# Second attention's first rows loaded within its projections, plain norms in two groups over eight banks, second chunk of each feed-forward turned later

## Time and profile before

| | |
|---|---|
| median of 3 runs | 1845.64 us (1845.48 to 1847.41) |
| profiled execution | 1844.86 us, span 1843.1 us |
| PE busy | 1647.8 us, 89% |
| DVE busy | 1372.2 us, 74% |
| ACT busy | 1104.0 us, 60% |
| POOL busy | 690.9 us, 37% |
| mean granted PE clock | 0.959 |

### The profile page before, as it was taken

One profiled execution on the slowest core, in us unless ns is written; L12 is line 12 of the kernel. 1 busy time (PEld: TensorE's weight loads), 2 busy tenths in 40 slices (PEclk: granted clock), 3 DMA queues, 4 the chain that ended last, 5 costly groups with the idle time before them and its releaser, 6 DMA issues. The chain is left out here.

```text
span 1843.1 us, 43046 instructions
## 1 busy us (share of the span) xinstructions
PE 1647.8 (89%) x14612; PEld 1021.5 (55%) x14612; DVE 1372.2 (74%) x2840; ACT 1104.0 (60%) x2096; POOL 690.9 (37%) x804
## 2 busy tenths in 40 slices
PE   2799999999999999999947664899999999985897
PEld 1477777787777778777724332233333333323555
DVE  4487887887788788778776574888888888846674
ACT  4566666666666666666646541366666666675452
POOL 0655554555555455555330432021212121223012
PEclk9999999999999999999979867899999999997999
DMA  4321121122112112211100020000000000000001
GB/s 129 96 56 44 43 54 40 43 48 54 43 43 54 40 43 48 52 44 34 24 1 1 6 101 12 15 14 14 15 14 15 14 15 14 10 1 1 1 12 35
DMA packets 53109, 61.86 MB, mean 34 GB/s; under 512 B 11345, under 2 KB 32018, under 8 KB 53010
## 3 DMA queue, kind: packets, MB, share of 16 engines
q1 hardware_dynamic: 53010, 60.55, 13.5%
HBM read 18.57 MB, written 2.10 MB: 11 GB/s over the span
## 5 line engine op out<-in xcount | busy, mean ns | idle before, releaser
L1732 ACT ACTIVATE a_prob<-psum 128x1024 f32<-128x1024 f32 (+3 forms) x384 | 302.3, 813 | 212.1 <-PE psum L1689 209.5
L1772 DVE TENSOR_REDUCE a_mx<-psum 128x1 f32<-128x512 f32 (+3 forms) x608 | 367.6, 655 | 61.5 <-PE psum L1671 55.6
L1764 POOL TENSOR_SCALAR_AFFINE_SELECT a_prob<-a_prob 128x256 f32<-128x256 f32 x256 | 103.9, 406 | 420.5 <-ACT a_prob L1732 418.1
L1668 PE MATMUL psum<-a_kd,a_qp 128*128 128x512 f16 (+3 forms) x768 | 218.3, 339 | 33.8 <-DMA a_kd<-a_k_part 23.0
L498 POOL TENSOR_TENSOR a_swp<-a_swp,a_sin 128x512 f32<-128x512 f32 x128 | 163.2, 1275 | 163.7 <-DMA a_swp<-a_lin 163.7
L854 DVE TENSOR_REDUCE a_nmax<-psum 128x1 f32<-128x1024 f32 (+7 forms) x256 | 191.4, 748 | 1.0 <-PE psum L569 1.0
L726 ACT ACTIVATE a_prob_big<-psum,a_nmax 128x1024 f32<-128x1024 f32 (+3 forms) x128 | 121.9, 953 | 103.3 <-DVE a_nmax L854 101.5
L502 POOL TENSOR_TENSOR a_rope<-a_swp,a_cosd 128x512 f32<-128x512 f32 x128 | 164.1, 1282 | 12.4 <-POOL a_swp L498 4.8
L1668 PEld LDWEIGHTS psum<-a_kd,a_qp 128*128 128x128 f16 x768 | 70.7, 98 | 173.9 <-DVE a_mx L1772 94.4
L1710 PE MATMUL psum<-a_prob,a_vg 128*32 128x512 f32 (+3 forms) x1536 | 165.4, 503 | 0.7 <-ACT a_o_sb L1738 0.3
L849 DVE TENSOR_TENSOR a_pt_lo_big<-psum,a_pt_hi_big 128x512 f16<-128x512 f32 (+3 forms) x256 | 138.5, 582 | 30.2 <-ACT a_pt_hi_big L721 30.2
(11 more groups left out here) (279 smaller groups left out, 4434.3 us busy)
## 6 DMA issues: line engine op xcount, KB each, us to landing
a_swp<-a_lin SPq DMA_DIRECT2D x256, 128.0 KB, 2.3
a_qp<-a_q_part SPq DMA_DIRECT2D x192, 16.0 KB
a_kd<-a_k_part SPq DMA_DIRECT2D x192, 16.0 KB
x<-_attn_hidden_states_dram SPq DMA_DIRECT2D x4, 512.0 KB, 5.6
a_w_raw<-in_L_attn_Wq_dram SPq DMA_DIRECT2D x16, 128.0 KB, 2.3
a_w_raw<-in_L_attn_Wk_dram SPq DMA_DIRECT2D x16, 128.0 KB, 2.3
a_w_raw<-in_L_attn_Wv_dram SPq DMA_DIRECT2D x16, 128.0 KB, 2.3
a_wo_raw<-in_L_attn_Wo_dram SPq DMA_DIRECT2D x1, 2048.0 KB
```

The costliest lines, as they stand in the source:

```text
L1668: last = pe.matmul(to[:, j * n:(j + 1) * n], qp[:, w % 3, t * P:(t + 1) * P], kd[:, w % 3, j0 + j, a:e], start=True, stop=not edge)
L1732: act.activation(prob_at(u, i)[:, 2 * pair:2 * pair + 2, a % BANK:a % BANK + e - a], c.psum[:, pair_of(u, i):pair_of(u, i) + 2, 0:e - a], ...
L1772: dve.tensor_reduce(mx[:, t, j0:j0 + per, a // BANK], work(("S", w, i))[:, 0:per * (e - a)].rearrange("p (j n) -> p j n", j=per), AX.X, AL ...
```

## The change

Three edits.

1. The 24 DMAs of unit 0 leave the attention block and are issued in the projections block, once the zeroing and the line of -1 are done and six low parts (those of sequence 0) are there. The attention block's SP loop begins at unit 1. `loaded_qk` is made earlier for that.
2. `boundary`, `Norm`, `run_steps` and the unused options of `Extra` go. The plain norms become `norm_and_turn`, written out without loops: the statistics chain runs for two groups, tiles 0 to 3 and tiles 4 to 15; each pair of tiles has a bank of its own, and the scaled tiles have four slots of two. `Moments`, which the feed-forwards already used, moves up in the file unchanged.
3. In chunk 0 of each feed-forward, the turn of chunk 1 with its high and low parts comes after ht = HT - 2 (4 in f0, 6 in f1) instead of ht = 2, on all three engines.

```diff
+    FIRST = TPC
+    NP = NT // 2
+        xn = c.sb(f"{name}_xn", [P, 4, 2, D], F32, ctx)
+        norm = Moments(c, name, [(0, FIRST), (FIRST, NT)], ctx)
...
+                norm.statistics(dve, c.x, 0, FIRST)
+                norm.variance(dve, 0)
+                norm.statistics(dve, c.x, FIRST, 2 * FIRST)
+                norm.normaliser(dve, 0)
+                norm.statistics(dve, c.x, 2 * FIRST, NT)
+                norm.variance(dve, 1)
+                norm.normaliser(dve, 1)
+                for m in range(NP):
+                    low(m)
...
+                def scale(m):
+                    act.wait_ge(norm.norm_ready, 2 if 2 * m < FIRST else 4)
+                    wait(act, turned, m - 3)
+                    for t in (2 * m, 2 * m + 1):
+                        act.activation(xn[:, m % 4, t % 2:t % 2 + 1, :], c.x[:, t:t + 1, :], ACT.Identity, ...)
...
+                norm.root(act, 0)
+                scale(0)
+                scale(1)
+                high(0)
+                high(1)
+                norm.root(act, 1)
+                for m in range(2, NP + 1):
+                    if m < NP:
+                        scale(m)
+                    if m >= 3:
+                        high(m - 1)
...
+                for m in range(NP):
+                    pe.wait_ge(xn_ready, 2 * m + 2)
+                    for j in range(2):
+                        for k in range(KT):
+                            last = pe.transpose(c.psum[:, m, k * 2 * P + j * P:k * 2 * P + (j + 1) * P],
+                                                xn[:, m % 4, j, k * P:(k + 1) * P], c.ident[:, :])
+                    last.then_inc(turned, 1)
...
+    TURN_AT = [HT - 2] + [2] * (CHUNKS - 1)
-                        if ht == 2 and ch + 1 < CHUNKS:
+                        if ht == TURN_AT[ch] and ch + 1 < CHUNKS:
...
+                @block.sync
+                def _(sp):
+                    sp.wait_ge(zeroed, 2)
+                    sp.wait_ge(lined, J)
+                    sp.wait_ge(lo_done, CB * NJ)
+                    load_rows(sp, 0)
...
-                    for u in range(NU):
+                    for u in range(1, NU):
...
+                        load_rows(sp, u)
```

More of the change, by code:

```diff
@@ L122, in wait, with __init__ @@
         eng.wait_ge(sem, value)
[L125 to L140, removed]
+class Moments:
     STEPS = 9
-    def __init__(self, c, name, ctx, unit=1.0):
-        self.eps = EPS * unit * unit
-        sb = lambda n, *shape: c.sb(f"{name}_{n}", [P, TPC, *shape], F32, ctx)
+    def __init__(self, c, name, groups, ctx, unit=1.0):
+        self.c, self.groups, self.eps = c, groups, EPS * unit * unit
+        sb = lambda n, *shape: c.sb(f"{name}_{n}", [P, NT, *shape], F32, ctx)
         self.stats = sb("stats", 6)
@@ L153, in __init__, with statistics, then_wait @@
             c.sem(f"{name}_{n}") for n in ("stats_ready", "step", "var_ready", "sd_ready", "norm_ready"))
-        self.c = c
-    def then_wait(self, dve, ch, k, ins):
+    def statistics(self, dve, src, t0, t1):
+        for t in range(t0, t1):
+            dve.bn_stats(self.stats[:, t, :], src[:, t:t + 1, :]).then_inc(self.stats_ready, 1)
+    def then_wait(self, dve, g, k, ins):
         ins.then_inc(self.step, 1)
[L158 to L174, removed]
-                                 op0=ALU.mult, op1=ALU.add).then_inc(self.var_ready, 1)
@@ L177, in root @@
[L177 to L191, removed]
+        dve.wait_ge(self.step, g * self.STEPS + k)
@@ new lines, in root, with normaliser @@
+    def root(self, act, g):
+        t0, t1 = self.groups[g]
+        act.wait_ge(self.var_ready, g + 1)
+        act.activation(self.sd[:, t0:t1], self.var[:, t0:t1], ACT.Sqrt).then_inc(self.sd_ready, 1)
+    def normaliser(self, dve, g):
+        t0, t1 = self.groups[g]
+        dve.wait_ge(self.var_ready, g + 1)
+        dve.wait_ge(self.sd_ready, g + 1)
+        self.then_wait(dve, g, 6, dve.reciprocal(self.inv[:, t0:t1], self.sd[:, t0:t1]))
+        self.then_wait(dve, g, 7, dve.tensor_tensor(self.quo[:, t0:t1], self.var[:, t0:t1], self.inv[:, t0:t1], ALU.mult))
+        self.then_wait(dve, g, 8, dve.tensor_tensor(self.avg[:, t0:t1], self.quo[:, t0:t1], self.sd[:, t0:t1], ALU.add))
+        self.then_wait(dve, g, 9, dve.reciprocal(self.half[:, t0:t1], self.avg[:, t0:t1]))
+        dve.scalar_tensor_tensor(out=self.shift[:, t0:t1], in0=self.msum[:, t0:t1], scalar=-1.0, in1=self.half[:, t0:t1],
@@ L202 @@
[L202 to L206 removed]
+    sync = gpsimd_first = lambda self, eng: None
 class Loads(Extra):
@@ L232, in _ @@
             @block.vector
             def _(dve):
[L234 to L253, removed]
@@ L254, in _, with low @@
-                run_steps(dve, X + 2, step)
-                dve.wait_ge(lo_ready, NT // GRP)
+                def low(m):
+                    dve.wait_ge(hi_ready, m + 1)
+                    dve.tensor_tensor(c.xT_lo[:, :, pair(m)], bank(m), c.xT_hi[:, :, pair(m)], ALU.subtract).then_inc(lo_ready, 1)
+                norm.statistics(dve, c.x, 0, FIRST)
+                norm.variance(dve, 0)
+                norm.statistics(dve, c.x, FIRST, 2 * FIRST)
+                norm.normaliser(dve, 0)
@@ L257, in _ @@
+                norm.statistics(dve, c.x, 2 * FIRST, NT)
[3 more added lines that the diff above has]
+                    low(m)
+                dve.wait_ge(lo_ready, NP)
             @block.scalar
             def _(act):
[L259 to L284, removed]
@@ L285, in _, with high @@
-                run_steps(act, X + 2, step)
+                def scale(m):
+                    act.wait_ge(norm.norm_ready, 2 if 2 * m < FIRST else 4)
+                    wait(act, turned, m - 3)
+                    for t in (2 * m, 2 * m + 1):
+                        act.activation(xn[:, m % 4, t % 2:t % 2 + 1, :], c.x[:, t:t + 1, :], ACT.Identity,
+                                       bias=norm.shift[:, t:t + 1], scale=norm.rstd[:, t:t + 1]).then_inc(xn_ready, 1)
+                def high(m):
+                    act.wait_ge(turned, m + 1)
+                    act.activation(c.xT_hi[:, :, pair(m)], bank(m), ACT.Copy).then_inc(hi_ready, 1)
@@ L287, in _ @@
+                norm.root(act, 0)
[9 more added lines that the diff above has]
+                        high(m - 1)
             @block.tensor
             def _(pe):
[L289 to L298, removed]
-                                last = pe.transpose(c.psum[:, g, k * GRP * P + j * P:k * GRP * P + (j + 1) * P],
-                                                    xn[:, g * GRP + j, k * P:(k + 1) * P], c.ident[:, :])
-                        last.then_inc(turned, 1)
```

122 lines of the change are left out of this document (37 added, 85 removed).

## The result

| | before | after |
|---|---|---|
| median (lowest to highest) | 1845.56 us (1841.25 to 1847.41, 4 runs) | 1821.67 us (1820.92 to 1822.38, 4 runs) |
| profiled execution, span | 1844.86 us, 1843.1 us | 1822.38 us, 1820.6 us |
| PE busy, mean granted clock | 89%, 0.959 | 91%, 0.962 |

The ratio is 0.9874, 95% interval 0.9856 to 0.9891. The forecast was 1821.7 us for the median. For the profiled execution it was 1821.0, and 1822.38 came.

What follows compares the result with a forecast made beforehand. PE at 89% busy bounds the kernel, so edits pay only where PE idles between stages. Gains 14.1 + 8.6 + 0.5 + 0.7 = 23.9 us give 1821.0 profiled, 1821.7 median; own range 1818.5 to 1825, 8-in-10 range 1815.5 to 1827.5.

Steps and rivals of the forecast that it cites:

- Part 1: Unit 0's 24 row loads issued during the second attention's projections: SP ends 2.9 us past DVE, gain 14.1 us.
- One sign of being wrong: For the moved loads: issue period beside the projections isn't 0.67, or next block opens other than 0.9 us after SP.
- The lower bound: For the moved loads: block's end also waits for the landing, next block opens at 1132.6, gain 13.2 us.
- The upper one: Best case for the moved loads: SP done before DVE, issues under 0.55, gain 17.4 us.
- Rivals B: Second attention's head: SP's early loads only move the wait; at 0.8 us per issue gain 11, time 1825; 8%.
- C: Norms gain, loads don't, as SP's wait passes only at the block's end: 9.8 us gain, time 1836; 3%.
- D: Issues stretch beside the projections: whole change a loss above 1.67 us each, 1850 us at 1.85 each; 2%.
- Part 2: The two plain norms in the new order, ACT the bound of the second group: 4.3 us gain each, 8.6 both.
- Part 3: Chunk 1 turned later in chunk 0 of both feed-forwards: gain 0.5 us in f1, 0.7 in f0.
- The text's own sign of being wrong: For the later turn in the feed-forwards: PE waits for low(1) at the start of chunk 1.
- the middle: f1's forecast gain of 0.5 us, taken between 1.4 gain at full clock and 0.4 loss if the clock has fallen.
- Rival A: Second attention's opening runs at another clock: up to 5 us, so 1817 or 1827; 20%, half to either side.

Runs made afterwards that it cites:

- after again: The changed kernel run and profiled once more, unchanged: 1819.53 us, ratio 0.9861 to the kernel before.

## Why the prediction was right

*Part 1* held to a tenth: 14.1 forecast, 14.13, 14.14 and 14.14 in three kernels. The start (1105.79 against "near 1105"), the period of 0.67 and the late one (SP, not DVE) were as written. One sign of being wrong did show, and hid in the sum: the next block opened 0.76 us behind SP, not 0.9, and the scan came 0.63 behind that, not 0.5. The lower bound did not occur: the block did not wait for the last landing, only the scan did. The upper one, 17.4, "SP done before the DVE", was reached and passed by the kernel with the earlier order (18.42 - 0.54 = 17.9). Rivals B, C and D, longer issues, loads that don't move or a late unit 1, did not happen; unit 1's first scan stands 25.53 us behind unit 0's, against 25.40 before.

*Part 2* came out 0.65 us better than my sum, 9.24 against 8.6. The size was off, not the mechanism: the second scaling started 9.8 us into the stage instead of 10.1, and a pair took 1.46 instead of 1.48 with 0.1 less in each hand-over. 0.62 us of idle time stand ahead of DVE's normaliser, which is the root behind high(1), as I had said.

*Part 3* had 0.7 for f0 and 0.5 for f1. f0 gave 0.95 in this profile; its down(0) came 46.8 to 46.9 us from the stage's start in five of the six profiles with the late turn but without the edit of ACT's scaling (48.5 in the other, with a low clock ahead of it), and at 47.7 to 47.9 in three without. So "PE's clock has no say in it" was wrong in one of six. f0 as a whole took 119.7 to 119.9 us in the three and 117.6 to 118.8 in the six, a gain of 0.9 to 2.3, so 0.7 was on the low side. The text's own sign of being wrong, a wait of PE for low(1) at the start of chunk 1, stands in f0's timeline after:
```profile
978.51 0.39 PE L1057 MATMUL psum<-xT_hi,ternary 128*128 128x512 f16 x1 [2.70 <-DVE xT_lo L1181]
```
It is what the layout had said for f0, with DVE as the bound: chunk 1 starts 43.4 us into the stage, where 981.4 - 938.14 = 43.3 was forecast (before, f0 began at 938.14). The sign was put too broadly; the step it stood for held. f1 gave nothing. My two ends were +1.4 at full clock and -0.4 at low clock. Its down(0) started at 55.0 to 55.5 us in three profiles with the old order, and at 54.5 to 56.0 in six with the new one, the spread being how long the half rate lasted around gate_up(0,4). So the bounds were sound, but "the middle" was too kind: the wait of 3.2 to 3.7 us ahead of gate_up(0,4) let the clock fall in each of the six; in the three kernels where it is 0.95 to 0.97 the clock stayed. The low stretch was only moved, from the turn to gate_up(0,4). The real fault there, ACT's scaling ahead of sigmoid(2), had been in my text as "set by ACT's scaling of chunk 1 and stays as it was", and I left it at that.

*Rival A* is where the text was weakest. I gave it 20% and 5 us to either side as if it were a property of the new kernel. Over the twelve profiles, old and new, the executions differ by 3.4 us in the second attention's opening and by 2.7 in the first's, and the changed kernel's two by 1.2 at f0's end. In the profiled pair it was 1.7 against the change, which is why that execution was 1.4 over its forecast while the medians met it. The end of f0 shows it in two lines, PE's last 38 matmuls after, and after again:
```profile
1038.10 5.99 PE L1072 MATMUL psum<-ternary,f_hidT 128*128 128x256 f16 x38 [0.40 <-DVE f_hidT L1201]
```
```profile
1039.64 4.32 PE L1072 MATMUL psum<-ternary,f_hidT 128*128 128x256 f16 x38 [0.40 <-DVE f_hidT L1201]
```
The waits ahead of the two are the same, 0.69, 1.03 and 0.40. The Trainium skill (TensorE: Matmul & The Clock Gate, part 1, the HAM clock gate) says that the number of matmuls at the lower rate at a kernel's start varies from run to run, that the ramp is under 1% of a typical span, and that one shouldn't fit to a specific count. The pairs agree, and show the same in the middle of a kernel: same program, other clock. One such place costs under 1% of the span, but here that is as large as a whole part of the change.

That the median met the forecast to 0.03 us is partly luck: part 2's surplus (0.65) and part 3's deficit (1.2 forecast, 0.76 come) nearly cancel, and the medians of the same kernel in two rounds of runs were 1821.67 and 1819.53.

## What to carry to other kernels

Issues on one queue are serial work with a length of their own, 0.67 us each here. Put them where another engine is busy, in the order in which their sources get ready, and check that the queue ends before that engine does. When a wait can't be shortened, look at what stands ahead of its releaser on the in-order engine: one line moved on ACT was worth more than the whole later turn. And compare kernels by stage from their profiles before comparing medians: the norms repeated to 0.06 us over the profiles, and the step from last low part to first scan to 0.02 in the five with the change's own order of the loads (18.01 to 18.42 in the three without), where whole runs of one kernel spread over 1 to 8.

## What the hardware showed that I had not expected

The granted clock can differ between two executions of one program at the same place, after the same waits, and at each of four such places this made a difference of 1.0 to 1.9 us between the changed kernel's two profiles. The 38 added matmuls of 256 columns, whose result nobody reads, went with a clock that stayed at full rate through the second attention's opening in both kernels that had them, where it fell in all ten without. The spread of the runs can't be laid to the kernel: 17 runs of the kernel before lay within 8.2 us on one chip and nine within 1.1 on another, where four of the kernel with the later loads spread over 4.9; the changed kernel's eight lay within 3.7.
